# A shorter top-k threshold search, silu on the scalar engine and another order of the work ahead of the scans

## What is computed

```python
x = x + sparse_attention(group_norm(x))    # scores of 1024 x 1024; each row keeps its 102 largest
                                           # (KEEP = int(0.1 * 1024)), then softmax, then values
t = tokens(x)
u = layer_norm(t)                          # eps 1e-5, and inside the block a second layer norm
t = t + (mamba_fwd(ln(u)) + mamba_bwd(ln(u)) + u)
t = t + moe(layer_norm(t))                 # 8 experts, 2 of them weighted per token

def mamba(x):                              # 256 inner channels (2 blocks of 128), 16 states
    xs, z = split(x @ in_proj.T)
    xs = silu(conv4(xs) + conv_b)          # a causal convolution of 4 taps
    dt = softplus((xs @ x_proj.T)[:16] @ dt_proj.T + dt_b)
    h[t] = exp(dt * A) * h[t-1] + dt * B * xs      # a scan over the tokens for each state
    y = sum_s(h * C) + xs * D
    return (y * silu(z)) @ out_proj.T
```

## Time and profile before

| | |
|---|---|
| median of three runs | 1622.19 us |
| the profiled execution | 1619.43 us, of which the span is 1617.7 us |
| VectorE (DVE) busy | 81% of the span |
| TensorE (PE) busy | 78% |
| ScalarE (ACT) busy | 57% |
| GpSimd (POOL) busy | 57% |

### The profile page before, as it was taken

The page is one execution under the profiler, slowest core; times in us unless marked ns, Lnnn a source line. Parts: engine busy times, 40 slices in busy tenths (PEclk is TensorE's granted clock), DMA queues, the critical chain, the costliest instruction groups (busy, mean ns, idle before and its releaser), DMA issues. The chain is left out here.

```text
span 1617.7 us, 17563 instructions
## 1 busy us (share of the span) xinstructions
PE 1255.3 (78%) x4450; PEld 644.4 (40%) x4450; DVE 1310.6 (81%) x1519; ACT 916.9 (57%) x1270; POOL 924.1 (57%) x487
## 2 busy tenths in 40 slices
PE   3308788898865778889973879888986668888868
PEld 1106253343525344334441625343452624434343
DVE  2785899998697699999678589999869678999930
ACT  1705767575644566666481575757564565656712
POOL 2122568787181547868345257878618164887834
PEclk8658789999987879999996878999998786999989
DMA  2000012221020012222021011222102001222203
GB/s 71 13 1 1 30 52 101 81 91 65 32 87 14 2 41 91 91 85 92 20 92 40 1 30 52 104 78 91 65 26 80 14 2 47 88 101 78 91 14 118
DMA packets 30498, 91.92 MB, mean 57 GB/s; under 512 B 4790, under 2 KB 8764, under 8 KB 30428
## 3 DMA queue, kind: packets, MB, share of 16 engines
q1 hardware_dynamic: 30428, 91.10, 16.2%
HBM read 88.34 MB, written 2.75 MB: 56 GB/s over the span
## 5 line engine op out<-in xcount | busy, mean ns | idle before, releaser
L637 POOL TENSOR_TENSOR work<-expo,ring 128x1024 f32<-128x1024 f32 x128 | 299.9, 2363 | 126.6 <-DVE expo L1295 124.6
L637 POOL TENSOR_TENSOR ring<-ring 128x1024 f32<-128x1024 f32 x128 | 299.8, 2365 | 9.8 <-DVE ring L1295 9.8
L1295 DVE TENSOR_TENSOR_SCAN expo<-ring,ps 128x1024 f32<-128x1024 f32 x128 | 286.0, 2270 | 0.0
L1745 PE MATMUL ps<-ring,ident 128*128 128x512 f32 x512 | 262.5, 617 | 28.0 <-POOL ring L637 21.5
L1295 DVE TENSOR_TENSOR_SCAN ring<-ring,ps 128x1024 f32<-128x1024 f32 x128 | 284.1, 2261 | 0.0
L1745 PE MATMUL ps<-work,ident 128*128 128x512 f32 x512 | 241.1, 593 | 0.0
L887 ACT ACTIVATE ring<-dt_f,decay 128x1024 f32<-128x1024 f32 x128 | 146.6, 1148 | 105.4 <-DVE expo L1295 61.5
L681 ACT ACTIVATE b_dtx_tok<-dtx_tok,b_tok 128x256 f32<-128x256 f32 x448 | 189.2, 493 | 0.0
L1708 PE MATMUL ps<-ident,b_dtx_tok 128*128 128x128 f32 x896 | 122.2, 279 | 46.4 <-DVE expo L1295 42.3
L1708 PEld LDWEIGHTS ps<-ident,b_dtx_tok 128*128 128x128 f32 x896 | 95.9, 140 | 138.8 <-issue 69.6
L1745 PEld LDWEIGHTS ps<-ring,ident 128*128 128x128 f32 x512 | 82.8, 189 | 166.2 <-POOL ring L637 128.1
(11 more groups left out here) (271 smaller groups left out, 2243.2 us busy)
## 6 DMA issues: line engine op xcount, KB each, us to landing
ring<-c_rows SPq DMA_DIRECT2D x128, 512.0 KB, 3.5
b_dtx_tok<-comb_rows SPq DMA_DIRECT2D x32, 512.0 KB, 3.6
x_c<-in_x SPq DMA_DIRECT2D x4, 512.0 KB, 3.3
out<-xs_f SPq DMA_DIRECT2D x4, 512.0 KB, 2.6
w<-in_L_ffn_w SPq DMA_DIRECT2D x2, 512.0 KB
ring<-in_L_attn_f_in_proj_w SPq DMA_DIRECT2D x1, 256.0 KB
ring<-in_L_attn_b_in_proj_w SPq DMA_DIRECT2D x1, 256.0 KB
c_rows<-dbc_f SPq DMA_DIRECT2D x4, 64.0 KB, 1.9
```

The lines of the kernel that those rows point to most:

```text
L637: pool.tensor_tensor(hc[odd][:, k, :], hs[odd][:, k, :], c_all[:, odd, :], ALU.mult).then_inc(hc_ready, 1)
L1295: v.tensor_tensor_scan(hs[odd][:, k, order], dA[:, k, order], dbu[:, order], 0.0, ALU.mult, ALU.add).then_inc(scan_ready, 1)
L1745: last = mm(halves(ps[2 * k])[h], ident[:, :], hc[odd][:, k, h * BANK:(h + 1) * BANK], start=False, stop=stop)
```

## The change

- **Search.** `DAMPING` goes; `first_correction` moves the threshold by the whole error, `second_correction` by the error times |d1| / (|d1| / 0.8 + |d2|), where d1 and d2 are the two errors. So there are two counting rounds that correct, on half the tiles each, and no round of VectorE's for the mask: ScalarE counts below for all 8 tiles (`count_last`, `copy_base`), and VectorE makes the low scores of tiles 4 to 7 itself (`lower`), with a compare and product in one instruction. GpSimd masks tiles 0 to 3. The ladder takes tiles 4 to 7 first, and `ranks` moves behind it. `select` runs for five experts before the first mask instead of four.
- **Conditional blocks.** The block for "none missed" stands first.
- **Norms.** `norm_variance` makes the inner and the outer variance at once, from var and var * (1 + eps) + eps * eps, and GpSimd raises both to the power in one instruction per half.
- **Preparation.** silu is ScalarE's own function: `conv_silu` and `z_gate` take the place of tanh, copies and products, with a load of its table in the middle of the norms. softplus becomes max(v, ln(1 + exp(min(v, 16)))): `cap_step` and `time_step` on VectorE, no `dt_abs`, `dt_positive`, `dt_sum`. The order of the steps is new on all engines; the last reader of the dt projection is now `time_step`.

```diff
-    DAMPING = (1.0, 0.6, 0.5)
-    COUNTS = len(DAMPING) + 1
+    SECANT = 0.8
+    COUNTS = 3
...
+        ladder_order = list(range(ACT_TILES, TILES)) + list(range(ACT_TILES))
+        low_scores = [(expo[:, 0, :], expo[:, 1, :], work[:, 0, :], work[:, 1, :])[j % 4] for j in range(TILES)]
...
-        conv_ps = ((ps23, ps67), (ps01, ps45))
-        z_ps = ((ps01, ps45), (ps67, ps01))
+        conv_ps = ((ps23, ps67), (ps45, ps01))
+        z_ps = ((ps01, ps01), (ps45, ps01))
...
-                    pool.tensor_tensor(ln_rstd[:, t], ln_var[:, t], neg_half[:, t], ALU.pow).then_inc(rstd_ready, 1)
-                    pool.wait_ge(var2_ready, 2 * b + half + 1)
-                    pool.tensor_tensor(ln_rstd2[:, t], ln_var2[:, t], neg_half[:, t], ALU.pow).then_inc(rstd2_ready, 1)
+                    pool.tensor_tensor(norm_rstd[:, :, t], norm_var[:, :, t], neg_half[:, :, t],
+                                       ALU.pow).then_inc(rstd_ready, 1)
...
-                    for x in range(4):
+                    for x in range(5):
                         select(m, x)
-                for j in range(TILES):
-                    mask_score(b, j)
-                    if m is not None and j % 2 == 1:
-                        select(m, 4 + j // 2)
+                mask_score(b, 0)
+                mask_score(b, 1)
+                if m is not None:
+                    select(m, 5)
+                    select(m, 6)
+                mask_score(b, 2)
+                mask_score(b, 3)
+                if m is not None:
+                    select(m, 7)
...
-                gates(b, 0)
-                gates(b, 1)
...
+            def count_last(b, tiles):
+
+                act.wait_ge(thresh_ready, (b + 1) * COUNTS)
+                for i in tiles:
+                    nc.scalar.activation(below[i], score[:, i, :], ACT.Sign, bias=thresh[:, i:i + 1], scale=-1.0,
+                                         accum_out=count[:, i:i + 1]).then_inc(counted, 1)
...
+                    if half == 0:
+                        nc.scalar.preload_act_table_set("silu_and_others")
...
-                z_parts(b, 0, 0)
-                conv_tanh(b, 0, 0)
-                z_parts(b, 0, 1)
+                z_gate(b, 0, 0)
                 conv_tap(b, 1, 0)
-                conv_tanh(b, 0, 1)
+                conv_silu(b, 0, 0)
+                z_gate(b, 0, 1)
+                conv_silu(b, 0, 1)
                 conv_tap(b, 1, 1)
-                z_parts(b, 1, 0)
                 b_and_c(b, 0)
-                dt_abs(b, 0, 0)
-                conv_tanh(b, 1, 0)
+                conv_silu(b, 1, 0)
+                z_gate(b, 1, 0)
                 middle_part(b, 0)
-                dt_abs(b, 0, 1)
-                z_parts(b, 1, 1)
-                conv_tanh(b, 1, 1)
+                conv_silu(b, 1, 1)
+                z_gate(b, 1, 1)
 
                 nc.scalar.preload_act_table_set("natural_log_exp_and_others")
                 dt_log(b, 0, 0)
+                dt_log(b, 0, 1)
                 b_and_c(b, 1)
...
+                link(v.tensor_tensor(thresh[:, :], delta[:, :], thresh[:, :], ALU.add))
+
+            def second_correction(b):
+
+                correct(b, 1)
+                v.tensor_tensor(moves[:, :], delta[:, :], first_move[:, :], ALU.mult)
+                link(v.scalar_tensor_tensor(weight[:, :], delta[:, :], -1.0, delta[:, :], ALU.mult, ALU.max))
+                link(v.scalar_tensor_tensor(weight[:, :], first_move[:, :], 1 / SECANT, weight[:, :], ALU.mult,
+                                            ALU.add))
+                link(v.reciprocal(weight[:, :], weight[:, :]))
+                link(v.tensor_tensor(moves[:, :], moves[:, :], weight[:, :], ALU.mult))
+                link(v.tensor_tensor(thresh[:, :], moves[:, :], thresh[:, :], ALU.add))
+                dve.sem_inc(thresh_ready, 1)
+
+            def lower(b):
+
+                for n, j in enumerate(range(ACT_TILES, TILES)):
+                    v.scalar_tensor_tensor(low_scores[j], score[:, j, :], thresh[:, j:j + 1], score[:, j, :],
+                                           ALU.is_lt, ALU.mult).then_inc(lowered, 1)
...
+            def cap_step(b, d, k):
+
+                g = (b * DIRS + d) * BLOCKS + k
+                dve.wait_ge(dt_filled, g + 1)
+                dve.wait_ge(xs_ready, g + 1)
+                v.tensor_scalar(soft_log[d][:, k, :], dt_ps[d][k][:, :], dt_b[:, d, k:k + 1], DT_LINEAR, ALU.add,
+                                ALU.min).then_inc(capped_ready, 1)
+
+            def time_step(b, d, k):
+
+                g = (b * DIRS + d) * BLOCKS + k
+                dve.wait_ge(log_ready, g + 1)
                 dve.wait_ge(dA_ready, b * UNITS)
...
+                v.scalar_tensor_tensor(dt[d][k], dt_ps[d][k][:, :], dt_b[:, d, k:k + 1], soft_log[d][:, k, :], ALU.add,
+                                       ALU.max).then_inc(dt_ready, 1)
...
+                convolve(b, 0, 1)
                 convolve(b, 1, 0)
+                convolve(b, 1, 1, range(1, 2))
                 rest(b, 0)
...
+                convolve(b, 1, 1, range(2, TAPS))
+                cap_step(b, 0, 0)
+                cap_step(b, 0, 1)
                 last_part(b, 0)
...
+                time_step(b, 0, 0)
                 dtx_forward(b, 0)
+                time_step(b, 0, 1)
+                dtx_forward(b, 1)
+                products(b, 0, 0, 0, 0, first=True)
                 rest(b, 1)
...
+                cap_step(b, 1, 0)
+                cap_step(b, 1, 1)
+                scan_product(b, 0, 0, 0, 0, 0, 0, first=True)
                 last_part(b, 1)
...
+                time_step(b, 1, 0)
                 scan_product(b, 0, 0, 0, 0, 0, 1, first=True)
...
+                time_step(b, 1, 1)
                 second_state(b, 0)
...
-                    pe.wait_ge(relu_ready, b * DIRS * BLOCKS + 4)
+                    pe.wait_ge(dt_ready, b * DIRS * BLOCKS + 4)
...
+                project_z(b, 1, 0)
                 project_z(b, 1, 1)
                 project_dbc(b, 1, 0)
                 project_dbc(b, 1, 1)
+
+                pe.wait_ge(parts_ready, b * DIRS + 1)
+                pe.wait_ge(mid_ready, b * DIRS + 1)
+                pe.wait_ge(dt_ready, b * DIRS * BLOCKS + 2)
+                spread(b, 0, 0, 0, first=True)
                 project_dt(b, 1, 0)
                 project_dt(b, 1, 1)
```

More of the change, by code:

```diff
@@ L252, in hybrid_block @@
         counted = sem("counted")
-        ranked = sem("ranked")
+        base_copied = sem("base_copied")
+        lowered = sem("lowered")
         masked = sem("masked")
@@ L1060, in count_above @@
                                          ALU.is_ge, ALU.add, accum_out=count[:, i:i + 1]))
-            def count_below():
-                for i in range(ACT_TILES, TILES):
-                    after()
-                    step(v.tensor_scalar(below[i], score[:, i, :], thresh[:, i:i + 1], None,
-                                         ALU.is_lt, ALU.add, accum_out=count[:, i:i + 1]))
             def correct(b, c):
                 after(0)
-                dve.wait_ge(counted, (b * COUNTS + c + 1) * ACT_TILES)
+                dve.wait_ge(counted, b * COUNTED + (c + 1) * ACT_TILES)
                 v.scalar_tensor_tensor(delta[:, by_sign], count[:, by_sign], N - 2 * TARGET,
@@ L1101, in next_below @@
                     after()
[L1102 to L1105 removed]
+                    step(v.match_replace(low_scores[j], ladder[:, j, 1:9], low_scores[j], REPLACED))
+                for n in pair:
+                    j = ladder_order[n]
+                    after(pair[1] - n)
+                    v.max(ladder[:, j, 9:17], low_scores[j]).then_inc(laddered, 1)
```

272 lines of the change are left out of this document (104 added, 168 removed).

## The result

| | median us | runs | span of the profiled execution | granted TensorE clock, mean |
|---|---|---|---|---|
| before, beside it | 1622.35 | 1621.81 to 1623.28 | 1617.7 | 0.892 |
| changed kernel | 1601.25 | 1599.37 to 1604.47 | 1602.7 | 0.887 |

The ratio is 0.9873 [0.9861, 0.9886]: 21.1 us less by the medians, 15.0 by the two profiled executions, of which that of the changed kernel was the slowest of its four. Forecast were 23.8 us less and 1598.4.

The account below looks back on a forecast made before the run. VectorE bounds the scans, elsewhere the chain that ends last. Search 7.0 + 13.4, blocks 10.4, norms 7.0, preparation -14.0 make 23.8 us, so the median 1622.19 becomes 1598.4; range for 8 in 10: 1582 to 1614.

Parts of the forecast that it names:

- the 0.35 us in the norms: First half's norm: with steps taken out, VectorE delivers the last softmax tile 0.35 us sooner per image.
- Search: First count to ladder: fewer counting rounds gain 7.0 us in image 0 and 13.4 in images 1 to 3.
- Blocks: Ahead of the first softmax product: 2.93 us of passing over the long block falls to 0.3, gaining 10.4 us.
- Norms: Norm coefficients: one power for two gains 1.4 us, an earlier last softmax tile 0.35, per image; 7.0 us in all.
- Table load: Loading silu's table while ScalarE waits for the norm coefficients costs nothing.
- Preparation: Second half's scaling to second pair of products: `token_major` waits for ps45's later last reader, a loss of 14.0 us.
- VectorE is full: Preparation, first `time_step` to release of ps45: VectorE works without a wait for 19.9 us, ending at X + 55.7.
- The first: Preparation gets shorter, the stage ending 4 to 6 us sooner: 20 us more gain, 1578; chance 14%.
- The second: Port contention eats the search gain (-9) and the jump stays (-10): 1617 with both, 1608 with one; chance 16%.
- The jump's half of it: Conditional blocks: entering a block costs as much as passing one, so the jump's gain is lost (-10).
- The third: Search: a row misses the window and its tile takes the exact search, 42 us more, 1640; chance 7%.
- The fourth: Preparation: the wait for ps45 comes 6 us later per image, with The second in full: 1630; chance 3%.

Follow-up runs that it names:

- the ordered kernel: Changed kernel in which GpSimd's selects 2 to 7 wait until VectorE's four `lower` are done: 1590.54 us, ratio 0.9797.
- the run with a missed row: Changed kernel with the flag of tile 0 set in every image, so the exact search runs once per image: 1760.08 us, ratio 1.0858.
- the six products: Changed kernel plus six unread products of x into ps01 ahead of `spread`, where TensorE waits for the first time steps: 1595.11 us, ratio 0.9833.

## Why the prediction was right, and where not

The time, 1601.25, is 2.9 us over the forecast and well in its range, and every mechanism of the forecast but one (the 0.35 us in the norms) was found in the trace. Term by term, X being the start of ScalarE's scaling of the second half, as in the prediction:

- **Search, 20.4 net of the rank step: 19.3.** Image 0 has the 18.05 that was summed (18.2). In images 1 to 3 I put the ladder at 25.0; it came at 26.34, 24.44 and 26.25. The step that was off is what lies in the shared queue: I had the rest of select 1 and selects 2 and 3, and let select 4 be the bound (27.4). Select 4 started at 454.49, inside of the four `lower`. In image 2 it starts later, beside the last `lower`, and waits itself (836.00, 3.39 us): that image has the 24.44. The rank step cost 0.28, not 0.45. That the claim at the port was the cause, and not something else of images 1 to 3, the ordered kernel shows: 20.1 to 20.5. The rule of the Trainium skill that I set beside it (SBUF — State Buffer, Who interferes with whom) agrees with the trace for the selects: the engine that started first holds on, in both directions (a select of 3.38 us, small steps of 2.05 and 2.18). For GpSimd's powers it holds in one direction only: a softmax product that starts within a power keeps its 1.28 us (the run with a missed row). That an instruction with the same tile on both inputs might need only one read is refuted by `lower`, 4.58 us for two.
- **Blocks, 10.4: 11.7,** and 11.5 as an edit by itself. The 0.3 that I left in front was too much: entering the first block leaves no idle time.
- **Norms, 7.0: 5.3.** The scaling's part is right: 1.5 per image, forecast 1.4. The step that failed is the 0.35 us by which VectorE was to deliver the last softmax tile sooner. I took three steps out of its list, and did not ask when the power is done that the next one waits for. It starts beside a softmax product, lasts 2.61 in place of 1.65, and VectorE stands 0.87 ahead of the last tile. The last softmax product starts 20.16 / 20.91 / 20.72 / 20.20 us behind the first one, where it was 20.27 / 20.53 / 19.67 / 20.50: 1.0 us later in four images, and not 1.4 sooner. The trace of before had the sign of it: there a power of four columns lasts 1.98 us beside a softmax product (521.48, image 1), and 1.01 alone. Moving the coefficients one tile back gave 0.7 to 1.0 in images 1 to 3.
- **Table load, 0: 0.** ScalarE still waits 1.03 us behind it. The figure of the Trainium skill (ScalarE: Activation LUTs, What ACT_TABLE_LOAD costs), about 2.66 us with the drain, isn't what this case shows: 1.28 apart.
- **Preparation, -14.0: -17.8,** the term that was mis-sized most. Its structure held: one wait, and 11.5 us behind it, the same in both kernels. Its start held too: the first time step came at X + 34.1 (556.00 - 521.90), 1.7 sooner than laid out. What was off is the 19.9 us of "VectorE is full" up to the release (the steps listed there make 20.05): it took 22.5, as VectorE waited 2.13 for the second block of the backward dt projection, which ran 7.19 us at half clock and for which I had no wait. The release came at X + 56.6, not 55.7. I had given TensorE's clock its place behind the wait, and not ahead of it. With TensorE's idle time filled the wait went in two images and halved in the other two.
- **Rivals.** The first (the preparation gets shorter) was wrong for the code as it stands: one wait did hold 11.5 us. That it becomes true with that wait undone is the largest finding here, 31.7 us. The second held in part, since select 4 fell in. The jump's half of it was refuted by the two blocks exchanged alone. The third didn't happen (no exact search in the trace), and its price of 42 was 39.7: 1 us more for the search, 4.5 less for the flags, 1.2 for the jump. The fourth: the release came 0.9 later, not 6.
- **The sum by traces,** 23.8 against 17.9 in the stages, is off by 3.8 in the preparation, 1.7 in the norms, 1.1 in the search and 0.7 in the scans' stretch, and by 1.3 the other way in the blocks. That 1601.25 comes within 2.9 of the forecast is in part luck: the medians put the gain at 21.1, the stages of the two traces at 17.9.

What stays open: what the token copies cost at the full clock, since nothing tried brought them there, and what sets when the clock falls within the dt projection (with the six products added, VectorE still waited in images 0 and 2, in 1 and 3 it didn't).

## What to carry to other kernels

When a change moves the last reader of a buffer, ask what now stands between its inputs and that read: here two scans and the third part of B and C stood in front of 11.5 us of a chain that needs the buffer, and two copies of 1.27 us took 8.5 us per image off a stage that the change had made 4.5 longer. Put the likelier of two conditional blocks first, whatever else is planned. And where two engines share a port, give the one on the path its turn by a semaphore: the other's delay of 6 us cost 0.5 us in four images, where 16.0 were won.

## What the runs showed of the hardware

- Passing over a long conditional block costs VectorE 2.8 to 3.0 us, entering one that comes first nothing that can be seen, and passing over the shorter of the two at most 1.19 (with a flag load).
- A power of eight columns on GpSimd lasts 2.61 us in place of 1.65 when it starts just behind a large VectorE instruction with two SBUF inputs. The other way round nothing is held: such an instruction that starts 0.39 us behind a power keeps its 1.28 us. A select of 128 x 1024 does hold VectorE, down to steps of four columns (2.05 us in place of 0.16).
- Three table loads in a row start 1.28 to 1.29 us apart.
- TensorE's granted clock fell from 1.00 to 0.50 with TensorE idle (changed kernel, 557, idle since 554.40) and also with TensorE busy (with the six products, 560, busy since 557.34). The backward dt projection took 7.19 us at 0.50 and 4.33 with most of it at 1.00.
- Behind 2.69 us of idling in place of 1.14 four products of x took 3.78 us at 0.50 in place of 2.84 at 0.68, and the first dt projection came 19.2 to 19.6 us behind the scaling in place of 18.4 to 18.6: part of a wait on another engine is paid for a second time in TensorE's clock.
